# Output slots of eight channels, stored as 48 and 9 rows every second step, and filter tables issued from ScalarE's queue

## The reference

```python
def layer1(x, conv_w, conv_b):
    g = _gn(x)                                                      # group norm over pairs of channels
    feat = jnp.einsum('bihw,oi->bohw', g, conv_w) + conv_b[None, :, None, None]   # pointwise, 32 to 32
    filt = jnp.einsum('kh,bchw,lw->bckl', Ph, feat, Pw)             # 5x5 bin means of each channel
    inp = feat.reshape(1, B * C, H, W)
    w = filt.reshape(B * C, 1, K, K)
    out = jax.lax.conv_general_dilated(inp, w, window_strides=(1, 1), padding=p,
                                       feature_group_count=B * C)   # each channel with its own 5x5 filter
    return x + out.reshape(B, C, H, W)
```

## Time and profile before

| | us |
|---|---|
| median of 3 runs | 5975.08 |
| lowest and highest | 5948.3, 5999.08 |
| the profiled execution, its own time | 5946.39 |
| the profiled execution, its span | 5944.8 |
| first store of the second layer issued at | 2445.5 |
| last store of the second layer issued at | 5937.2 |

### The profile page before, as it was taken

One profiled execution on the slowest core, in us unless ns is written; L12 is line 12 of the kernel. 1 busy time (PEld: TensorE's weight loads), 2 busy tenths in 40 slices (PEclk: granted clock), 3 DMA queues, 4 the chain that ended last, 5 costly groups with the idle time before them and its releaser, 6 DMA issues.

```text
span 5944.8 us, 108642 instructions
## 1 busy us (share of the span) xinstructions
PE 5164.0 (87%) x43848; PEld 3729.7 (63%) x43848; DVE 4578.8 (77%) x5377; ACT 4027.8 (68%) x2541; POOL 1191.9 (20%) x735
## 2 busy tenths in 40 slices
PE   1989898989989894699799799799899799799798
PEld 0434343434434342588688788788788688688688
DVE  6989898989989866677577677677677678577576
ACT  2767676675767672677577677677677678577675
POOL 0000000000000001133233233233233233233233
PEclk9999999999999997899899899899999899899899
DMA  7979798988879664899999999999999999999997
GB/s 273 390 286 403 289 372 320 359 332 332 360 295 395 251 248 124 144 175 169 174 173 169 175 172 172 177 171 168 178 174 172 176 174 173 171 175 176 171 175 126
DMA packets 1311457, 1353.69 MB, mean 228 GB/s; under 512 B 542778, under 2 KB 1101114, under 8 KB 1233722
## 3 DMA queue, kind: packets, MB, share of 16 engines
q0 software_dynamic: 667008, 540.98, 43.0%
q1 hardware_dynamic: 624034, 660.56, 40.2%
q10 hardware_dynamic: 19872, 144.71, 6.1%
HBM read 803.24 MB, written 538.84 MB: 226 GB/s over the span
## 4 chain that ended last, share of the span: by engine, by line
DMA 35%; SPq 13%; DVE 5%; PE 3%; issue 3%; ACT 1%; POOLq 0%; ACTq 0%; DVEq 0%; POOL 0%
DMA out_dram<-c_xr 27%; SPq L869 11%; DMA c_x<-out_dram 6%; PE c_tps L1163 3%; SPq L975 2%; DVE c_xr L1124 2%; DMA c_tt<-bias_scratch 2%; DVE c_z L1090 2%; DVE c_feat L1117 1%; ACT c_xr L1080 0%; ACT c_z L1058 0%; PE c_cps L1142 0%; PE c_cps L1144 0%; PE c_cps L1143 0%; ACT c_feat L1071 0%
## 5 line engine op out<-in xcount | busy, mean ns | idle before, releaser
L1163 PE MATMUL c_tps<-c_feat,c_tt 123*128 123x256 f16 (+1 forms) x20736 | 2432.4, 276 | 363.6 <-DMA c_tt<-bias_scratch 180.1
L1163 PEld LDWEIGHTS c_tps<-c_feat,c_tt 123*128 123x128 f16 (+1 forms) x20736 | 2017.0, 99 | 664.9 <-issue 146.5
L508 PE MATMUL b_ps<-b_xq,w0main 128*128 128x512 bf16 x9168 | 2002.7, 381 | 150.1 <-ACT b_haloq L442 150.1
L508 PEld LDWEIGHTS b_ps<-b_xq,w0main 128*128 128x128 bf16 x9168 | 891.9, 97 | 1256.0 <-ACT b_haloq L442 131.2
L1017 POOL DMA_DIRECT2D out_dram<-c_xr x576 | 1098.0, 1906 | 2511.6 <-DVE c_xr L1124 1982.2
L1124 DVE TENSOR_SCALAR c_xr<-c_tps 57x1024 f32<-57x1024 f32 (+1 forms) x576 | 699.3, 1214 | 838.4 <-DMA out_dram<-c_xr 558.6
L1058 ACT ACTIVATE c_z<-c_x,c_rs 128x976 f16<-128x976 f32 x576 | 1152.0, 2000 | 237.8 <-DMA c_x<-out_dram 153.0
L1090 DVE SCALAR_TENSOR_TENSOR c_z<-c_x,c_rs,c_z 128x976 f16<-128x976 f32 x576 | 1104.3, 1917 | 124.8 <-ACT c_z L1058 109.6
L1080 ACT ACTIVATE c_xr<-c_tps 57x1024 f32<-57x1024 f32 (+1 forms) x576 | 636.9, 1106 | 812.8 <-DMA out_dram<-c_xr 537.1
L450 ACT ACTIVATE b_q<-b_ps,q_bias 128x1024 int8<-128x1024 f32 x512 | 567.2, 1109 | 600.2 <-PE b_ps L508 570.8
L1142 PE MATMUL c_cps<-w_high,c_z 128*128 128x128 f16 x4608 | 806.9, 220 | 64.7 <-DVE c_z L1090 43.5
(11 more groups left out here) (140 smaller groups left out, 1399.3 us busy)
## 6 DMA issues: line engine op xcount, KB each, us to landing
out_dram<-b_x POOLq DMA_DIRECT2D x128, 2048.0 KB, 8.0
out_dram<-c_xr POOLq DMA_DIRECT2D x512, 456.0 KB, 19.5
c_x<-out_dram SPq DMA_DIRECT2D x224, 976.0 KB, 26.3
b_stream<-in_x_dram SPq DMA_DIRECT2D x168, 1024.0 KB, 10.0
b_x<-in_x_dram ACTq DMA_DIRECT2D x138, 1024.0 KB, 9.1
b_x<-in_x_dram SPq DMA_DIRECT2D x138, 1024.0 KB, 8.9
c_tt<-table_scratch SPq DMA_DIRECT2D x64, 576.0 KB
c_x<-out_dram SPq DMA_DIRECT2D x32, 944.0 KB, 24.8
```

What stands on the lines that cost most here:

```text
L508: last = pe.matmul(ps[:, g % 3, j, :], k.w0main[:, y, d, :, :].rearrange("p o r -> p (o r)"), row(2 * i + j + y - 1)[:, d:d + W], start=(y ...
L1163: last = pe.matmul(tps[:, s % 2, o % 4, :], tt[0:rows, o, tp, 2 * d:2 * d + 2, :].rearrange("k w m -> k (w m)"), feat[0:rows, (e * N + i) ...
```

## The change

`c_xr` keeps its size but is cut into two slots of eight channels instead of four of four (`XR_SLOTS` = 2, `GATHER` = 2). A slot is filled by two steps. POOL's queue stores it after the second one, by two accumulating transfers: rows 0 to 47 and rows 48 to 56, eight channels each (in the last block 48 and 8 rows). Both add 16 to the slot's semaphore. ACT and DVE wait for a slot only in the first of its two steps. The tables are issued by ACT's queue: group g right behind the eviction of step 2g + 1 of an image's last block. SP's queue keeps the loads of x1, the last edge row of the bias, and the first image's tables.

```diff
-XR_SLOTS = 4
+XR_SLOTS = 2
+GATHER = 2
...
-        xr = sb("c_xr", [P, XR_SLOTS // 2, 4, W], F32)
+        xr = sb("c_xr", [P, 4 * GATHER, W], F32)
...
-        def xr_rows(m, lo, hi):
+        def xr_rows(m, lo, hi, o, channels):
...
-            base = PR * (m % XR_SLOTS % 2)
-            return xr[base + lo:base + hi, m % XR_SLOTS // 2, :, :]
+            base = PR * (m // GATHER % XR_SLOTS)
+            return xr[base + lo:base + hi, o:o + channels, :]
...
+        def load_table(eng, p, e, g):
+            for a in range(2):
+                for lo, hi in ((0, SPLIT), (SPLIT, ROWS_IN)):
...
+                    eng.dma_start(dst.rearrange("k o t w m -> k (o t w m)"), src).then_inc(t_loaded[g], 16)
+            eng.dma_start(tt[MAIN:EDGE + 1, 8 * g:8 * g + 8, :, :, :].rearrange("k o t w m -> k o (t w m)"),
+                         bias_d[0:2, e::2, :, :][:, p, 8 * g:8 * g + 8, :]).then_inc(t_loaded[g], 16)
...
-                    if pointwise and j == N and s in (2, 4):
-                        sp.wait_ge(band_done, count(p, e, TILES, TILES - STEPS + s) + START)
-                        load_table(p, e + 1, s // 2 - 1)
                     if s == 6 and pointwise and (j + 2 < N or another(p, e)):
                         load_x1(sp, p, e, j + 2)
-                    if pointwise and j == N and s == STEPS - 1:
-                        for g in (2, 3):
-                            sp.wait_ge(band_done, count(p, e, TILES, TILES - STEPS + 2 * g + 2) + START)
-                            load_table(p, e + 1, g)
...
+                    if s % GATHER != GATHER - 1:
+                        continue
                     pool.wait_ge(odd_out, count(p, e, TILES, m + 1) + START)
                     pool.wait_ge(even_out, count(p, e, TILES, m + 1) + START)
-                    pool.dma_start(out[e::2][p, 4 * s:4 * s + 4, r0:r0 + n, :].rearrange("c h w -> h c w"),
-                                   xr_rows(m, 0, n), accum_op=ALU.add).then_inc(stored[m % XR_SLOTS], 16)
+                    o = 4 * (s - GATHER + 1)
+                    for lo, hi in ((0, SPLIT), (SPLIT, n)):
+                        pool.dma_start(out[e::2][p, o:o + 4 * GATHER, r0 + lo:r0 + hi, :].rearrange("c h w -> h c w"),
+                                       xr_rows(m, lo, hi, 0, 4 * GATHER), accum_op=ALU.add).then_inc(stored[m // GATHER % XR_SLOTS], 16)
...
         def wait_slot(eng, p, e, m):
-            eng.wait_ge(stored[m % XR_SLOTS], count(p, e, TILES // XR_SLOTS * 16, m // XR_SLOTS * 16) + 16)
+            g = m // GATHER
+            eng.wait_ge(stored[g % XR_SLOTS], count(p, e, STORES // XR_SLOTS * 32, g // XR_SLOTS * 32) + 16)
...
-                        wait_slot(act, p, e, m)
+                        if s % GATHER == 0:
+                            wait_slot(act, p, e, m)
                         act.wait_ge(band_done, count(p, e, TILES, m + 1) + START)
                         res, conv = half_out(m, rows_out(j - 1), 1)
                         act.activation(res, conv, ACT.Identity, scale=1.0 / FS).then_inc(odd_out, 1)
+                        if pointwise and j == N and s % 2:
+
+                            load_table(act, p, e + 1, s // 2)
```

More of the change, by code:

```diff
@@ L902, in depthwise @@
         TILES = N * STEPS
-        assert TILES % XR_SLOTS == 0
+        STORES = TILES // GATHER
+        assert STORES % XR_SLOTS == 0
         last_rows = H - ROWS_OUT * (N - 1)
@@ L949, in loads_of @@
             return p * (N * Q * 16) + ((e * N + j) // 2 + 1) * (Q * 16)
+        def load_table(eng, p, e, g):
+            for a in range(2):
+                for lo, hi in ((0, SPLIT), (SPLIT, ROWS_IN)):
+                    src = table_d[e:nb:2][p, a, 8 * g * TROW + lo:8 * (g + 1) * TROW]
+                    src = bass.AP(tensor=src.tensor, offset=src.offset, ap=[[1, hi - lo], [1, 8 * TROW]])
+                    dst = tt[ROWS_IN * a + lo:ROWS_IN * a + hi, 8 * g:8 * g + 8, :, :, :]
+                    eng.dma_start(dst.rearrange("k o t w m -> k (o t w m)"), src).then_inc(t_loaded[g], 16)
+            eng.dma_start(tt[MAIN:EDGE + 1, 8 * g:8 * g + 8, :, :, :].rearrange("k o t w m -> k o (t w m)"),
+                         bias_d[0:2, e::2, :, :][:, p, 8 * g:8 * g + 8, :]).then_inc(t_loaded[g], 16)
         def load_x1(eng, p, e, j):
@@ L966, in load_last_edge @@
                              bias_d[2:3, e::2, :, :][:, p, :, :]).then_inc(edge_loaded, 16)
[L968 to L977, removed]
             def group(p, e, j, pointwise, banded):
@@ L981, in group @@
                     for g in range(4):
-                        load_table(p, e, g)
+                        load_table(sp, p, e, g)
                 for s in range(STEPS):
-                    if pointwise and j == N and s in (2, 4):
-                        sp.wait_ge(band_done, count(p, e, TILES, TILES - STEPS + s) + START)
-                        load_table(p, e + 1, s // 2 - 1)
                     if s == 6 and pointwise and (j + 2 < N or another(p, e)):
                         load_x1(sp, p, e, j + 2)
-                    if pointwise and j == N and s == STEPS - 1:
-                        for g in (2, 3):
-                            sp.wait_ge(band_done, count(p, e, TILES, TILES - STEPS + 2 * g + 2) + START)
-                            load_table(p, e + 1, g)
                     if banded and j == 3 and s == 2:
@@ L1014, in group @@
                     n, r0 = rows_out(j - 1), ROWS_OUT * (j - 1)
+                    if s % GATHER != GATHER - 1:
+                        continue
                     pool.wait_ge(odd_out, count(p, e, TILES, m + 1) + START)
                     pool.wait_ge(even_out, count(p, e, TILES, m + 1) + START)
-                    pool.dma_start(out[e::2][p, 4 * s:4 * s + 4, r0:r0 + n, :].rearrange("c h w -> h c w"),
-                                   xr_rows(m, 0, n), accum_op=ALU.add).then_inc(stored[m % XR_SLOTS], 16)
+                    o = 4 * (s - GATHER + 1)
+                    for lo, hi in ((0, SPLIT), (SPLIT, n)):
+                        pool.dma_start(out[e::2][p, o:o + 4 * GATHER, r0 + lo:r0 + hi, :].rearrange("c h w -> h c w"),
+                                       xr_rows(m, lo, hi, 0, 4 * GATHER), accum_op=ALU.add).then_inc(stored[m // GATHER % XR_SLOTS], 16)
             run(pool, group)
             for m in range(XR_SLOTS):
-                pool.wait_ge(stored[m], nb * (TILES // XR_SLOTS) * 16 + 16)
+                pool.wait_ge(stored[m], nb * (STORES // XR_SLOTS) * 32 + 16)
         def positions(e, j, part):
@@ L1041, in half_out @@
         def half_out(m, n, h):
-            return (xr_rows(m, 0, n).rearrange("h c (j p) -> h p c j", p=2)[:, 1 - h, :, :],
+            return (xr_rows(m, 0, n, 4 * (m % GATHER), 4).rearrange("h c (j p) -> h p c j", p=2)[:, 1 - h, :, :],
                     tps[PR * h:PR * h + n, m % 2, :, :])
         def wait_slot(eng, p, e, m):
-            eng.wait_ge(stored[m % XR_SLOTS], count(p, e, TILES // XR_SLOTS * 16, m // XR_SLOTS * 16) + 16)
+            g = m // GATHER
+            eng.wait_ge(stored[g % XR_SLOTS], count(p, e, STORES // XR_SLOTS * 32, g // XR_SLOTS * 32) + 16)
         @block.scalar
@@ L1120, in group @@
                         m = STEPS * (j - 1) + s
-                        wait_slot(dve, p, e, m)
+                        if s % GATHER == 0:
+                            wait_slot(dve, p, e, m)
                         dve.wait_ge(band_done, count(p, e, TILES, m + 1) + START)
```

## The result

| | before | after |
|---|---|---|
| median, us | 5977.76 (4 runs) | 5674.03 (4 runs) |
| lowest and highest, us | 5948.3, 5999.08 | 5671.45, 5677.44 |
| ratio, 95% interval | | 0.9495, 0.9454 to 0.9537 |
| profiled execution, its own time, us | 5946.39 | 5672.2 |
| second layer, first to last eviction on DVE, us | 3492.1 | 3212.9 |

The changed kernel is 5.0% faster: 5674 us where 5530 was forecast, inside the range. The last two rows are made from the times at which DVE's evictions into `c_xr` start, one for each of 576 steps: a steady step is the mean interval over blocks 1 to 7 of images 1 to 6 (336 intervals), and the excess is what the 16 steps around each of the seven image changes (block 8 and the next image's block 0) take beyond 16 steady ones.

A forecast was written before the change was run, and what follows sets the result against it. The prediction took steady steps as held up by stores on three engines, with DMA share 1.00; stores 380 us plus tables 35 gave 415, 5946 - 415 = 5531, say 5530 us, range 5310 to 5780.

The forecast's parts named there:

- Three engines under each store: Second layer's stores: 57 rows use 3 engines, 1232 packets; split 48 and 9, two steps have 544 packets instead of 2464.
- The slots' round in the kernel before: Steady steps before: four slots with eviction, POOL's wait and 19.7 us of store come round in 21.5 us, 5.4 a step.
- The floor of computation, 4.43 us: Steady steps: computation alone needs 4.43 us, as stores follow each other by 4.3 to 4.5 us where nothing stalls.
- the value of 5.00: Steady step after the change: taken as 5.00 us, between 4.43 and 5.07, near the DMA end.
- the term of 380 us: Stores' gain over the second layer: 576 steps x 0.66 us = 380 us, with ends 340 and 708.
- Rival A: Steady steps: DMA engines give way, latency of 3-engine stores was the bound; 5140 us for all, 5330 halfway; chance 0.24.
- The DMA engines at 5.07: Steady steps: if the DMA engines are the bound, fewer empty packets bring a step from 5.66 to 5.07 us.
- Slots: Two slots of two steps: landing 7.6 us for 48 rows, 10.3 with the second part, inside 11.5 us.
- Cost nothing: The fewer, larger slots were priced at nothing; if 1 us over, 288 x 1 us.
- rival B: Slots: late stores stop ACT and DVE for two steps; 6420 us, milder form 6030; chance 0.05.
- Tables: Seven image changes: ACT's queue ends PE's 180.1 us wait; at most 66 us gained, 35 taken; ACT's issues uncovered +81.
- Rival C: Steady steps: nothing changes, 5.66 us stays, image changes give some 35: 5910 us; chance 0.11 with weak gains.

The follow-up runs named there:

- slots_only: The changed kernel with the tables left on SP's queue, as before the change: 5658.66 us, ratio 0.9501 to the kernel before.
- split_only: The kernel before, four slots of four channels, each stored as 48 and 9 rows, tables on SP's queue: 5631.29 us, ratio 0.9461.

## Why the prediction was right, and where not

The measured 5674 us lies in the range, and the reason that the prediction gives for the gain, a store on too few engines, is right. Where in the range it lies owes something to luck: the prediction's two bounds of a step, 4.43 and 5.07, are both below what binds, and the result is near the upper end of its 4.85 to 5.3 a step.

*Three engines under each store.* Right. The packets on q0 came out exact for the changed kernel (175,424), and for the store in one piece (662,336) and that of 56 rows (175,488). 56 rows instead of 57 gave 319 us with nothing else changed.

*The slots' round in the kernel before.* In the main right: taking a product off TensorE left its step at 5.70, so stores set it, and the 21.5 us of round, 5.4 a step, come near. Not shown is that the round of the slots and not the DMA engines, at a share of 1.00 with the empty packets, holds that step. In the kernel with undivided stores of eight channels, where the share is 0.60, it is the round.

*The floor of computation, 4.43 us.* This step failed. It read the pace from the intervals between stores where nothing stalls, and these are intervals of catching up, on the engines that evict. TensorE's pace is 5.29: 36 banded matmuls in 3.95 to 4.0 us (DVE's last evictions of the changed program, where PE does nothing else, are 3.88 and 4.02 apart in turn) and 24 pointwise ones in 1.34. It could be read before: PE was busy for 300.70 us of 322 in 56 steps, 5.37 a step, with some of it at a granted clock below full (0.99 in the mean), and the argument never divided the two. So the value of 5.00 lay below a floor, and the term of 380 us was 576 x 0.42 = 242. Rival A, all of it, was excluded by the same row, and with it most of the range's lower part: even without any reload of tables the changed kernel took 5515 us.

*The DMA engines at 5.07.* It isn't what binds in the changed kernel. The mean of 5.12 where TensorE was relieved is close to it, but no run shows that the engines set it, and 30 steps in a row ran there at 4.85. The DMA share of 1.00 doesn't tell how near the engines are to being the limit: it is 0.97 in the changed kernel's steady part, too, where PE has no idle time.

*Slots.* The landing was forecast at 7.6 us for the 48-row part and 10.3 with the second behind it; measured 10.5 and 11.9. With steps of 5.29 the room is 3 x 5.29 - 1.8 = 14.1 us, so it is mostly hidden in the steady part, as said (8.6 us of 140 are left; from 3270 to 3570 us ACT waits 18.5 us for slots, where under 15 of 300 were forecast). At the image changes it isn't. Cost nothing was wrong there: rival B's mechanism, stores behind table packets, holds just in those blocks. That rival's 18 us for 24 packets beside the tables was even mild, since the slowest store lands after 27.8, and the mistake was to give it a chance for the whole kernel and none for its place. Against slots_only, measured beside them, four slots without such waits were 27 us faster and small pieces of table 41.

*Tables.* 35 us were forecast, half of the idle 66; the excess of the seven changes fell by 7 x 6.5 = 46 us. But the reason is not ACT's queue: with the tables left on SP's the excess is 25.4 as well. Each of the moves alone takes the excess to 25; together they take it no further, since the tables' transfers themselves are what costs there (2.5 without them). On ACT their issue isn't free: the next `c_feat` stood behind it for 22.0 us in all in the changed kernel (at most 81 were forecast), in exchange for PE's waits for tables, which are gone. And ACT's waits for loads of x1, which were to rise in the place of those for slots, fell from 153.0 to 32.4 us.

*The sum.* Forecast 380 + 35 = 415; measured 242 + 46 = 288 by these two terms, 274 in the profiled executions; most of the rest is in the last image, which gained 15 us over its last 64 steps where 0.42 each would be 27. POOL's issues, forecast at 2.1 us for two, took 1.95.

Rival C is out. The rule of the Trainium skill against two transfers in place of one (DMA: Bandwidth & Descriptors, "Rules for kernel authors") didn't hold here: split_only has 1152 transfers instead of 576 and is faster all the same; with 576 of 56 rows the ratio is 0.9465, with 1152 it is 0.9461. The rule compares halves that both use all engines; here the undivided store used three. Its section on the number of engines (same page, "Why a DMA increments its semaphore by 16 and not by 1") is what the packet counts agree with, by its divisor and not by its exception for some direct copies.

Open: how far the changed kernel could fall at image changes. The 23 us of a table reload are more than the 9 us of idle DMA that the old change had, and the study didn't separate what the engines need for the bytes from what the order of transfers costs.

## What to carry to other kernels

Count the packets of a transfer against its rows: a number of packets far above rows times pieces, in whole multiples, says that most engines only get empty ones (here 1232 packets for 228 pieces), and one row less, or the same rows in two parts with a good divisor, can be worth more than any new buffering. Before a term of a sum goes below the present step, divide each engine's busy time by the number of steps, PE's first: intervals between stores or evictions after a stall are catching up and no floor. Large pieces beside a store on another queue made it late (27.8 us at worst, 17.4 with small ones); cut the pieces, and expect little of the queue that issues them once the stores are spread.

## What was not expected of the hardware

With the stores spread, moving the tables from one queue to another changed nothing (0.9501 and 0.9495; 0.9425 and 0.9419), although in the second pair it turned PE's 92.7 us of waiting for tables into ACT's 107.1 us of waiting for x1; with stores on three engines the same move was worth 0.6%. The landing of the accumulating store grew with the packets on its busiest engine, by the reading above: 8.3 us in the median with 12 to 16, 10.5 with 24, 19.5 with 76, 30.6 with 152 of them. And a DMA share of 0.97 to 1.02 was seen with TensorE as the limit (5.29 us a step), with stores as the limit (5.71) and with TensorE relieved (5.12) alike, so that the share alone named none of them.
